# A three-layer decoder kernel: where it waits for the stored queries of its second attention, the order of that stage's first loads, and a wait of the experts' first transposes

## The chip, the cores and the metric

One Trainium2 chip, one core of it. The time is device microseconds (us) of one execution of the whole kernel, one launch. Engines: PE (TensorE), DVE (VectorE), ACT (ScalarE), POOL (GpSimd) and SP (SyncE, which here only issues DMAs and waits). The measured times of the kernel before are three, 1827.96 to 1846.97 us, so a difference below about 1% can hardly be told from none.

## The reference

`x` is 4 x 1024 tokens of 256 values, `ctx` is 4 x 77 tokens. All arithmetic is float32.

```python
x = layernorm(x + attn(x, ...))            # 16 heads of 16, rotary, ALiBi: causal bias only, softmax over 1024 keys
x = layernorm(x + xattn(x, ctx, mask, ...))
x = layernorm(x + ffn(x, ...))             # router, top 2 of 8 experts, 1024 places each, hidden 1024

def xattn(q, k, v, mask, ...):             # k = v = ctx
    qh, kh, vh = heads(q @ Wq.T + bq), heads(k @ Wk.T + bk), heads(v @ Wv.T + bv)
    scores = einsum('bhqd,bhkd->bhqk', qh, kh) / sqrt(16) + mask * -1e15
    return heads_back(softmax(scores) @ vh) @ Wo.T + bo

def ffn(x, ...):
    ids, probs = top2(relu(x @ rw1 + rb1) @ rw2 + rb2)
    disp = rows of x, sorted to their experts' places
    h = relu(einsum('enc,ech->enh', disp, ew1) + eb1)
    return sum over both experts of probs * (einsum('enh,ehc->enc', h, ew2) + eb2)
```

## The kernel before

The kernel is seven stages, one behind the other, each a block of five instruction streams, one for each engine. At the end of a block every engine drains (line 49 in the profile) and all wait for all; the next stage's instructions start behind that. Semaphores order everything else by hand: `eng.wait_ge(sem, value)` holds back all that follows on that engine, and a DMA raises its semaphore by 16 when it has landed.

The stages of the 4096 tokens: projections (`stage_qkv`), self attention, `stage_self_out` (output projection, norm, and the queries and keys of the second attention), `stage_cross` (the second attention, its projection and norm), router, `stage_experts`, `stage_combine`. From `stage_self_out` on they work in 8 chunks of 512 tokens.

**Queries through DRAM.** `stage_self_out` splits each chunk's queries into a high and a low part (`q_hi`, `q_lo`) and SP stores both to `q2_scr` (`store_q`, line 1156; the profile calls the tensor `q_scr`). Their landings are counted by `q_out[n % 2]`, 32 for each chunk. The x1 rows are stored at line 1151 (`x1_out`). The second attention loads a chunk's queries as a stack: `load_query_side` (line 1049) brings rows 0 to 47 of one half of the partitions, SP the one half and ACT the other. There are 4 such stacks; 0 and 1 are loaded in `stage_self_out` already. Each stack also has rows of ones (`load_ones`, line 1056, 64 KB a DMA, counted by `ones_in`).

**The second attention's start.** Scores are made twice. First `max_pairs` (line 1804): half a tile's heads each, 8 for a chunk, into PSUM, and DVE takes maxima (line 1708). When a chunk's 8 are there, DVE makes the negated maxima as two float parts (`shifts`), PE transposes them (line 1813), ACT copies them to `neg_t` (`copy_top`, line 1647), and SP moves them through DRAM to two rows of the query stack (`move_top`: store at line 1594, then loads at 1598). Only then can PE make that chunk's true scores (`scores`, line 1824), with the shift as rows of the product. Ahead of the main loop PE makes 14 such halves (`LEAD`), all of chunk 0 and 6 of chunk 1. The main loop then goes in 8 steps a chunk, with a `max_pairs` in each until all are made. SP's stream in the loop loads stack n + 3, x1 of chunk n (for the residual), moves the shift of n + 1 and stores chunk n - 2.

**The experts' start.** The router's last act on SP is to load the first two blocks of sorted rows (`first_rows`). In `stage_experts` SP loads the biases `eb1` (`b1`) and the constant `spare`, both counted by `const_in`. PE transposes the first rows (line 2465), ACT and DVE split them (2343, 2379), DVE works out shares and homes with `spare` (`shares`), and PE's products follow (2477). `b1` is first read by ACT's relus.

Of the kernel before, what the change touches and what calls it, by code (L numbers as in the profile page):

```python
# [13 lines left out]
F32R = mybir.dt.float32r  # L14
# [7 lines left out]
P = 128  # L22
# [4 lines left out]
CK = C // P  # L27
CH = 512
TPC = CH // P
CHUNKS = T // CH  # L30
# [85 lines left out]
PAIRS = H // 2  # L116
# [918 lines left out]
def cross_tiles(s):  # L1035

    return {"k_max": s.sb("k_max", [P, PAIRS, B, LP], F32R), "k_exp": s.sb("k_exp", [P, PAIRS, B, L], F32R),
            "v_all": s.sb("v_all", [L, B, H, VP], F32), "key_bias": s.sb("key_bias", [L, B], F32),  # L1040
            "stacks": [s.sb(f"q_stack{i}", [P, PAIRS, CH], F32R) for i in range(2)]}


def load_query_side(eng, io, n, side, stack):

    src = io["q2_scr"][n].rearrange("r (j s) t -> s r j t", s=2)[side]
    for row, first, last in ((0, 0, 2 * D), (2 * D, 0, D)):
        at = 64 * side + row
        eng.dma_start(stack[at:at + last - first, :, :].bitcast(F32), src[first:last]).then_inc(io["chunk_in"][n], 16)
# [12 lines left out]
Q_STORES = 32  # L1062
# [5 lines left out]
def stage_self_out(nc, io, pre, lent):  # L1068

    with Scope(nc, "so") as s:  # L1070
# [9 lines left out]
        q_sum = [s.sb(f"q_sum{i}", [P, CK, CH], F32) for i in range(2)]  # L1080
        q_hi = [s.sb(f"q_hi{i}", [P, CK, CH], F32R) for i in range(2)]
        q_lo = [s.sb(f"q_lo{i}", [P, CK, CH], F32R) for i in range(2)]
        norm = Norm(nc, s, io["apart"])
# [15 lines left out]
        spare = stacks[1][:, :, :].rearrange("p j t -> p (j t)")  # L1099
        wk_hi, wk_lo = [spare[:, i * 2048:(i + 1) * 2048].rearrange("p (c m) -> p c m", c=CK) for i in range(2)]  # L1100
        t_ps = s.pb("t_ps", (P, CK, CH))
        r_ps = s.pb("r_ps", (P, TPC, C))
# [8 lines left out]
        ones_in = lent["ones_in"]  # L1111
# [7 lines left out]
        x1_out = [s.sem(f"x1_out{i}") for i in range(2)]  # L1119
        q_out = [s.sem(f"q_out{i}") for i in range(2)]  # L1120
        block = s.block()
# [13 lines left out]
        def _(sp):  # L1135
# [44 lines left out]
            for c in range(2):  # L1180
                sp.wait_ge(x1_out[c], 16 * CHUNKS // 2)
                sp.wait_ge(q_out[c], Q_STORES * CHUNKS // 2)

# [335 lines left out]
def stage_cross(nc, io, pre, lent):  # L1519


    with Scope(nc, "cr") as s:
# [36 lines left out]
        x2_done = s.sem("x2_done")  # L1559
        ones_in = lent["ones_in"]  # L1560
        out_done = s.sem("out_done")
# [16 lines left out]
        def _(sp):  # L1578
            def load_stack(n):
                if n >= Q_SETS:  # L1580
                    sp.wait_ge(s_done, H * (n - Q_SETS) + H)
                load_query_side(sp, io, n, 0, qst[n % Q_SETS])

# [17 lines left out]
            def store(n):  # L1601
# [3 lines left out]
                sp.dma_start(chunk_rows(io["x2_scr"][0:T], n), x2[n % 2][:, :, :]).then_inc(out_done, 16)  # L1605

            load_stack(2)
            for i in (2, 3):
                load_ones(sp, io, qst[i], ones_in)
            load_x(0)  # L1610
            move_top(0)
            sp.dma_start(bo, io["bo"].partition_broadcast(P)).then_inc(weights_in, 16)
# [28 lines left out]
        def _(act):  # L1641
# [28 lines left out]
            def load_stack(n):  # L1670
                if n >= Q_SETS:
                    act.wait_ge(s_done, H * (n - Q_SETS) + H)
                load_query_side(act, io, n, 1, qst[n % Q_SETS])

# [27 lines left out]
        def _(dve):  # L1702
# [42 lines left out]
            for h in range(LEAD):  # L1745
                maxima(h)
                if h == HALVES - 1:
                    shifts(0)
            dve.wait_ge(hi_done, 1)
            nc.vector.tensor_tensor(wo_lo[:, :, :], wo_raw, wo_hi[:, :, :].bitcast(F32), ALU.subtract).then_inc(lo_done, 1)  # L1750
            for n in range(CHUNKS + 2):
                for u in range(HALVES):
                    h = HALVES * n + u + LEAD
# [28 lines left out]
        def _(pe):  # L1782
# [8 lines left out]
            def max_pairs(h):  # L1791
                n, q, b, t, first = max_half(h)
                if h % HALVES == 0:
                    pe.wait_ge(q_in[n], STACKED)
                    if n == 2:
                        pe.wait_ge(ones_in, 128)
                if 2 <= h < LEAD:
                    pe.wait_ge(m_free, h - 1)
                elif h >= LEAD:
                    pe.wait_ge(m_free, h)  # L1800
                for j in range(HG):
                    for side in range(2):
                        rows = slice(64 * side, 64 * side + ROWS_MAX)
                        ins = nc.tensor.matmul(max_bank(h)[:, side, j * LP:(j + 1) * LP], q[rows, first + j, t * P:(t + 1) * P],  # L1804
                                               k_max[rows, first + j, b, :], start=True, stop=True)
                ins.then_inc(m_full, 1)
# [416 lines left out]
def stage_experts(nc, io, keep):  # L2223

    with Scope(nc, "ex") as s:
# [100 lines left out]
        def _(act):  # L2326
            act.sem_inc(relu_done, 2)
            act.wait_ge(const_in, 32)

# [37 lines left out]

            split_x(0, 0)
            for e in range(E):
                expert(e, e % 2, e == E - 1)  # L2370

        @block.vector
        def _(dve):
# [7 lines left out]
            def shares(h, c):  # L2381
                e, at = h // 2, SHARE_STEPS * h
                who, home_of = rows[c][:, :, C:C + 1], rows[c][:, :, C + 2:C + 3]
                dve.wait_ge(in_done[c], 16 * e + 16)
                dve.wait_ge(ratio_done, h + 1)
                if h >= 4:
                    dve.wait_ge(added, 64 * (h - 3))
# [67 lines left out]
        def _(pe):  # L2455
            pe.sem_inc(h_done, 16)
            pe.wait_ge(const_in, 32)

# [316 lines left out]
```

## Time and profile before

| | us |
|---|---|
| median of 3 executions | 1835.07 |
| lowest, highest | 1827.96, 1846.97 |
| the profiled execution, its own time | 1830.21 |
| its span, first to last instruction | 1828.4 |
| second attention, first to last product of PE (about 1022 to 1220) | some 200 |
| experts (about 1394 to 1784) | some 390 |

The span is what the trace covers, 1.8 us less than that execution's own time. PE is busy for 89% of the span, but the stages differ, and a chain that ended last says little here, since it reaches back only into the last stage. So the two joints between stages that the change touches are read from the timelines.

### The profile page before, as it was taken

The numbers are of one execution on the slowest core, as the hardware profiler recorded it, in microseconds if no ns is written. First come the engines' busy times: TensorE is split into PE (matmuls) and PEld (weight loads), VectorE is DVE, ScalarE is ACT, GpSimd is POOL, SyncE is SP. The second block draws the span as 40 slices with busy tenths as digits, with TensorE's granted clock in tenths as the row PEclk, the third lists the DMA queues.
The fourth block names the chain that finished last, engine by engine and source line by source line (L and its number), as shares of the span: only waits on it lengthen the run. The fifth ranks groups of instructions, "written<-read, shape, count | busy, mean of one in ns | idle before, by whom it ended". The sixth has DMA issues, their size and how long they took to land. (4 is left out here: it accounts for less than half of the span.)

```text
span 1828.4 us, 36172 instructions
## 1 busy us (share of the span) xinstructions
PE 1623.4 (89%) x14816; PEld 1061.1 (58%) x14816; DVE 1278.5 (70%) x2240; ACT 1006.9 (55%) x1727; POOL 387.6 (21%) x265
## 2 busy tenths in 40 slices
PE   7869999999999999999777599869984999999990
PEld 6734444444444444444366455547763888888890
DVE  6978888888888888888177446752333677777744
ACT  5326777777777777777635267844532233333313
POOL 6550000000000000000014001101452355555521
PEclk9968999999999999999889578978996999999995
DMA  7955444443433343420238866223213244434226
GB/s 240 259 168 95 93 93 91 91 90 90 98 84 65 63 69 69 69 39 9 78 125 239 191 96 122 68 86 110 84 39 114 70 96 96 96 96 96 39 24 195
DMA packets 130388, 184.36 MB, mean 101 GB/s; under 512 B 29466, under 2 KB 93736, under 8 KB 129132
## 3 DMA queue, kind: packets, MB, share of 16 engines
q1 hardware_dynamic: 113456, 153.70, 34.0%
q0 software_dynamic: 13440, 22.07, 5.8%
q10 hardware_dynamic: 3328, 6.29, 2.1%
q8 instruction: 117, 1.92, 0.5%
q14 instruction: 47, 0.39, 0.1%
HBM read 115.32 MB, written 70.06 MB: 101 GB/s over the span
## 5 line engine op out<-in xcount | busy, mean ns | idle before, releaser
L734 DVE TENSOR_REDUCE att_row_max<-att_ring 128x2 f32<-128x1024 f32 x512 | 601.7, 1220 | 108.4 <-PE att_ring L799 76.4
L718 ACT ACTIVATE att_w_exp<-att_s_ps 128x512 f32<-128x512 f32 x1008 | 539.2, 598 | 210.1 <-PE att_s_ps L846 140.3
L873 PE MATMUL att_a_ps<-att_w_exp,att_v_group 128*32 128x512 f32 x2048 | 273.6, 606 | 0.8 <-ACT att_acc_sb L707 0.6
L832 PE MATMUL att_s_ps<-att_q_stack,att_k_stack 62*128 62x512 f32 x640 | 183.8, 478 | 0.0
L832 PEld LDWEIGHTS att_s_ps<-att_q_stack,att_k_stack 62*128 62x128 f32 x640 | 86.2, 184 | 122.2 <-ACT att_w_exp L718 111.9
L2357 ACT ACTIVATE ex_hid<-ex_h_ps,ex_b 128x512 f32<-128x512 f32 x128 | 87.4, 686 | 116.7 <-DVE ex_h_lo L2412 66.5
L2412 DVE TENSOR_TENSOR ex_h_lo<-ex_hid,ex_h_hi 128x512 fp32r<-128x512 f32 x128 | 138.6, 1083 | 4.4
L648 POOL COPY att_eyes<-keep_slope_eye 128x384 bf16<-128x384 bf16 x16 | 8.1, 507 | 622.6 <-PE att_s_ps L846 613.7
L2307 POOL DMA_INDIRECT x_scr<-ex_y,ex_home x60 | 100.6, 1677 | 176.0 <-DVE ex_y L2402 162.3
L846 PE MATMUL att_s_ps<-att_eyes,keep_past_bf 64*128 64x64 bf16 x3786 | 131.8, 193 | 0.0
L799 PE MATMUL att_ring<-att_k_stack,att_q_stack 60*128 60x512 f32 x640 | 125.6, 439 | 5.0 <-DVE att_row_max L734 4.1
L832 PE MATMUL att_s_ps<-keep_q_stack,keep_k_stack 62*128 62x512 f32 x368 | 109.4, 487 | 1.7 <-ACT att_w_exp L718 1.2
L846 PEld LDWEIGHTS att_s_ps<-att_eyes,keep_past_bf 64*128 64x128 bf16 x3786 | 92.1, 95 | 29.7 <-issue 17.7
L1656 ACT ACTIVATE cr_e<-cr_score_ps,pre_key_bias 77x512 f32<-77x512 f32 x128 | 80.5, 679 | 40.6 <-PE cr_score_ps L1824 39.8
L799 PE MATMUL att_ring<-keep_k_stack,keep_q_stack 60*128 60x512 f32 x384 | 85.6, 487 | 18.3 <-DVE att_row_max L734 8.9
L2343 ACT ACTIVATE ex_x_hi<-ex_t_ps 128x1024 fp32r<-128x1024 f32 x16 | 16.4, 1028 | 139.7 <-PE ex_t_ps L2465 139.7
L832 PEld LDWEIGHTS att_s_ps<-keep_q_stack,keep_k_stack 62*128 62x128 f32 x368 | 50.4, 188 | 73.9 <-ACT att_w_exp L718 67.8
L2410 DVE CAST ex_h_hi<-ex_hid 128x512 fp32r<-128x512 f32 x128 | 71.9, 562 | 15.8 <-ACT ex_hid L2357 15.1
L2420 DVE TENSOR_TENSOR ex_y<-ex_y_ps,ex_b 128x256 f32<-128x256 f32 x64 | 25.4, 420 | 80.5 <-PE ex_y_ps L2488 80.5
L1708 DVE TENSOR_REDUCE cr_top<-cr_m_ps 128x8 f32<-128x616 f32 x57 | 45.4, 797 | 48.8 <-PE cr_m_ps L1804 48.4
L807 PEld LDWEIGHTS att_ring<-att_eyes,keep_past_bf 64*128 64x128 bf16 x1280 | 35.1, 98 | 67.2 <-issue 67.2
L2488 PE MATMUL ex_y_ps<-ex_w_hi,ex_h_lo 128*128 128x256 f32 x256 | 72.9, 285 | 0.0
(314 smaller groups left out, 3552.6 us busy)
## 6 DMA issues: line engine op xcount, KB each, us to landing
first_w_raw<-ew SPq DMA_DIRECT2D x16, 1024.0 KB
att_k_stack<-qk_scr SPq DMA_DIRECT2D x40, 256.0 KB
rows_scr<-att_zeros POOLq DMA_DIRECT2D x8, 1040.0 KB, 9.3
first_rows<-rows_scr SPq DMA_DIRECT2D x16, 520.0 KB
qk_scr<-qkv_t_lo SPq DMA_DIRECT2D x14, 512.0 KB, 4.7
qk_scr<-qkv_t_hi SPq DMA_DIRECT2D x14, 512.0 KB, 4.4
keep_k_stack<-qk_scr SPq DMA_DIRECT2D x24, 256.0 KB
att_q_stack<-qk_scr SPq DMA_DIRECT2D x20, 256.0 KB
```

What stands on the lines that cost most here:

```text
L718: nc.scalar.activation(w_exp[(STEPS * g.n + st) % SETS][h][:, :], score_bank(v), ACT.Exp).then_inc(exp_done, 1)
L734: nc.vector.tensor_reduce(out, ring[place.slot][:, :, :], AX.X, ALU.max).then_inc(ring_free, 1)
L799: return nc.tensor.matmul(ring[place.slot][:, i, :], qs[g.buf][rows, j, tok:tok + P], ks[g.buf][rows, half, j, kk * CH:(kk + 1) * CH], sta ...
L832: ins = nc.tensor.matmul(score_bank(v), ks[g.buf][rows, c, j, kt * P:(kt + 1) * P], qs[g.buf][rows, j, c * CH:(c + 1) * CH], start=True, s ...
L846: ins = nc.tensor.matmul(bank[:, at:at + 64], past[side, far, half, :], eyes[g.buf][side, part, h // 2, :], start=False, stop=n == last)
L873: ins = nc.tensor.matmul(a_ps[32 * h:32 * h + 32, :], vg[g.buf][:, kt, h * VW:h * VW + 32], w_exp[(STEPS * g.n + st) % SETS][h][:, :], sta ...
L1656: nc.scalar.activation(e[p % E_SETS][:, side, :], s_ps[v % S_BANKS][0:L, :], ACT.Exp, bias=key_bias[:, n // 2:n // 2 + 1]).then_inc(exp_do ...
L2307: pool.indirect_dma_start(io["x2_scr"], bass.IndirectOffsetOnAxis(home[h % 4][:, t, :], 0), y[c][:, t, :], None, compute_op=ALU.add).then_ ...
L2357: nc.scalar.activation(hid[m % 2][:, :], h_ps[m % 2][:, :], ACT.Relu, bias=b1[:, bass.ds(e, 1), m:m + 1].rearrange("p a b -> p (a b)") if ...
L2410: nc.vector.tensor_copy(h_hi[c][:, m, :], hid[m % 2][:, :]).then_inc(h_hi_done, 1)
L2412: nc.vector.tensor_tensor(h_lo[c][:, m, :], hid[m % 2][:, :], h_hi[c][:, m, :].bitcast(F32), ALU.subtract).then_inc(h_lo_done, 1)
L2488: ins = nc.tensor.matmul(y_ps[t][:, 0:C], a, b, start=(j == 0), stop=(j == len(prods) - 1))
```

## The change

Four things, in two stages.

1. `q_out` is made in `cross_tiles` and lives on in the second attention. `stage_self_out` no longer ends with a wait of SP for it; instead SP and ACT wait for it in `load_stack`, for the chunk that they load, and DVE waits for all of it once, ahead of `wo_lo`. `q_hi` and `q_lo` stand later in the list of buffers, so that what the second attention writes first does not lie on them.
2. On SP, at that stage's start, the ones of stack 2 and `move_top(0)` stand ahead, and the ones of stack 3 and x1 of chunk 0 behind them.
3. PE waits for the ones of stacks 2 and 3 apart.
4. In `stage_experts` PE no longer waits for `const_in`; ACT waits for it behind its first split, DVE in `shares`.

```diff
@@ cross_tiles
-            "stacks": [...]}
+            "stacks": [...],
+            "q_out": [s.sem(f"q_out{i}") for i in range(2)]}
@@ stage_self_out
-        q_hi = [s.sb(f"q_hi{i}", [P, CK, CH], F32R) for i in range(2)]
-        q_lo = [s.sb(f"q_lo{i}", [P, CK, CH], F32R) for i in range(2)]
...
+        q_hi = [s.sb(f"q_hi{i}", [P, CK, CH], F32R) for i in range(2)]
+        q_lo = [s.sb(f"q_lo{i}", [P, CK, CH], F32R) for i in range(2)]
...
             for c in range(2):
                 sp.wait_ge(x1_out[c], 16 * CHUNKS // 2)
-                sp.wait_ge(q_out[c], Q_STORES * CHUNKS // 2)
@@ stage_cross, SP (ACT's load_stack alike)
             def load_stack(n):
                 if n >= Q_SETS:
                     sp.wait_ge(s_done, H * (n - Q_SETS) + H)
+                sp.wait_ge(q_out[n % 2], Q_STORES * (n // 2 + 1))
                 load_query_side(sp, io, n, 0, qst[n % Q_SETS])
...
+            load_ones(sp, io, qst[2], ones_in)
             load_stack(2)
-            for i in (2, 3):
-                load_ones(sp, io, qst[i], ones_in)
+            move_top(0)
+            sp.wait_ge(ones_in, 96)
+            load_ones(sp, io, qst[3], ones_in)
             load_x(0)
-            move_top(0)
@@ stage_cross, DVE
                 if h == HALVES - 1:
                     shifts(0)
+
+            for c in range(2):
+                dve.wait_ge(q_out[c], Q_STORES * CHUNKS // 2)
             dve.wait_ge(hi_done, 1)
@@ stage_cross, PE, max_pairs
-                    if n == 2:
-                        pe.wait_ge(ones_in, 128)
+                    if n in (2, 3):
+                        pe.wait_ge(ones_in, 32 * n + 32)
@@ stage_experts
             act.sem_inc(relu_done, 2)
-            act.wait_ge(const_in, 32)
...
             split_x(0, 0)
+            act.wait_ge(const_in, 32)
...
                 dve.wait_ge(ratio_done, h + 1)
+                if h == 0:
+                    dve.wait_ge(const_in, 32)
...
             pe.sem_inc(h_done, 16)
-            pe.wait_ge(const_in, 32)
```

The order on SP's queue, from the last store of queries over the end of the stage (the two branches) into the second attention. `cr_q_stack` are stacks 2 and 3, `pre_q_stack` stacks 0 and 1. Before:

```order
L1156 DMA q_scr<-so_q_lo 128x2x512
L49 UNCONDITIONAL_BRANCH [waits so_x1_out1,so_q_out0,so_q_out1,so_x1_out0,lent_ones_in]
L1577 UNCONDITIONAL_BRANCH [waits barrier_Pool_Activation_PE_DVE_SP_release]
L1049 DMA cr_q_stack<-q_scr 32x8x512
L1049 DMA cr_q_stack<-q_scr 16x8x512
L1056 DMA cr_q_stack<-ones_scr 4x4096 x4
L1589 DMA cr_x<-x_scr 128x4x256
L1594 DMA shift_scr<-cr_neg_t 32x512 [waits cr_top_copied]
L1598 DMA pre_q_stack<-shift_scr 2x4096 [waits cr_top_out]
L1598 DMA pre_q_stack<-shift_scr 2x4096
L1612 DMA lent_att<-bo 128x256
L1049 DMA cr_q_stack<-q_scr 32x8x512
```

and in the changed kernel (whose lines have numbers of their own):

```order
L1158 DMA q_scr<-so_q_lo 128x2x512
L49 UNCONDITIONAL_BRANCH [waits so_x1_out1,so_x1_out0,lent_ones_in]
L1578 UNCONDITIONAL_BRANCH [waits barrier_Pool_Activation_PE_DVE_SP_release]
L1057 DMA cr_q_stack<-ones_scr 4x4096 x2
L1050 DMA cr_q_stack<-q_scr 32x8x512 [waits pre_q_out0]
L1050 DMA cr_q_stack<-q_scr 16x8x512
L1596 DMA shift_scr<-cr_neg_t 32x512 [waits cr_top_copied]
L1600 DMA pre_q_stack<-shift_scr 2x4096 [waits cr_top_out]
L1600 DMA pre_q_stack<-shift_scr 2x4096
L1057 DMA cr_q_stack<-ones_scr 4x4096 [waits lent_ones_in]
L1057 DMA cr_q_stack<-ones_scr 4x4096
L1591 DMA cr_x<-x_scr 128x4x256
L1615 DMA lent_att<-bo 128x256
```

The waits for the queries' stores have left the stage's end, and the shift's store has moved ahead of two ones loads and of x1's load.

The order on PE where the experts begin, before:

```order
L2454 UNCONDITIONAL_BRANCH [waits barrier_Pool_Activation_PE_DVE_SP_release]
L2465 MATMUL ex_t_ps<-lent_ident,first_rows 128x128 [waits first_rows_in0,ex_const_in]
L2465 MATMUL ex_t_ps<-lent_ident,first_rows 128x128 x7
L2465 MATMUL ex_t_ps<-lent_ident,first_rows 128x128 [waits ex_x_lo_done,first_rows_in1]
L2465 MATMUL ex_t_ps<-lent_ident,first_rows 128x128 x7
```

and in the changed kernel:

```order
L2463 UNCONDITIONAL_BRANCH [waits barrier_Pool_Activation_PE_DVE_SP_release]
L2473 MATMUL ex_t_ps<-lent_ident,first_rows 128x128 [waits first_rows_in0]
L2473 MATMUL ex_t_ps<-lent_ident,first_rows 128x128 x7
L2473 MATMUL ex_t_ps<-lent_ident,first_rows 128x128 [waits ex_x_lo_done,first_rows_in1]
L2473 MATMUL ex_t_ps<-lent_ident,first_rows 128x128 x7
```

Nothing has changed its place; the first transpose waits for the rows alone.

## Rows read from the trace of the kernel before

**Rows 1.** The page's first line.

```profile
span 1828.4 us, 36172 instructions
```

**Rows 2.** Timeline of SP: start us, us, line, operation (instructions in a row).

```profile
1015.21 0.47 SPq L1156 DMA_DIRECT2D q_scr<-so_q_lo  x1
1022.06 1.22 SPq L1049 DMA_DIRECT2D cr_q_stack<-q_scr  x2
...
1025.05 0.39 SPq L1589 DMA_DIRECT2D cr_x<-x_scr  x1
1033.02 0.32 SPq L1594 DMA_DIRECT2D shift_scr<-cr_neg_t  x1
1040.67 0.53 SPq L1598 DMA_DIRECT2D pre_q_stack<-shift_scr  x2
...
1041.65 1.20 SPq L1049 DMA_DIRECT2D cr_q_stack<-q_scr  x2
...
1093.80 0.31 SPq L1594 DMA_DIRECT2D shift_scr<-cr_neg_t  x1
...
1118.75 0.33 SPq L1594 DMA_DIRECT2D shift_scr<-cr_neg_t  x1
...
1139.13 0.33 SPq L1594 DMA_DIRECT2D shift_scr<-cr_neg_t  x1
```

**Rows 3.** Timeline of PE and ACT: in brackets idle before, and its releaser.

```profile
1022.10 1.08 PE L1804 MATMUL cr_m_ps<-pre_k_max,pre_q_stack 52*128 52x78 f32 x8 [13.28 <-PEq L49]
...
1032.40 0.59 ACT L1647 ACTIVATE cr_neg_t<-cr_turn_ps 32x512 fp32r<-32x512 f32 x1 [18.89 <-PE cr_turn_ps L1813]
...
1038.21 1.07 PE L1804 MATMUL cr_m_ps<-pre_k_max,pre_q_stack 52*128 52x78 f32 x8 [0.90 <-DVE cr_top L1708]
...
1044.86 0.71 PE L1824 MATMUL cr_score_ps<-pre_q_stack,pre_k_exp 50*77 50x512 f32 x2 [5.57 <-DMA pre_q_stack<-shift_scr]
```

**Rows 4.** Waits of SP, 1000 to 1024 us: total, times, longest.

```profile
SPq L1181 <- DMA q_scr<-so_q_lo: 3.4, 1, 3.4
...
SPq L1182 <- DMA q_scr<-so_q_lo: 2.5, 1, 2.5
```

**Rows 5.** Landings of the last x1 store (L1151), issued at 1000.5.

```profile
DMA to landing us min/median/max: 9.2/9.2/9.2
```

**Rows 6.** Line 49, a stage's end: 1012 to 1023, then 1380 to 1392.

```profile
L49 DVEq DRAIN  x1: 1258/1258/1258, 1013.6 to 1013.6; - x1
...
L49 POOLq DRAIN  x1: 5284/5284/5284, 1386.2 to 1386.2; - x1
```

**Rows 7.** Landings of the shift's stores (L1594), and of x loads (L1589).

```profile
DMA to landing us min/median/max: 2.2/5.1/7.6
...
DMA to landing us min/median/max: 3.6/8.2/15.4
```

**Rows 8.** DMA queue q1, 1038 to 1041: packets, MB, share of 16 engines.

```profile
q1 hardware_dynamic: 112, 0.11, 11.8%
```

**Rows 9.** Timeline of SP and PE where the experts begin.

```profile
1391.77 0.35 SPq L2263 DMA_DIRECT2D ex_b<-eb  x1
1392.17 0.42 SPq L2264 DMA_DIRECT2D ex_spare<-spare  x1
...
1394.02 1.97 PE L2465 MATMUL ex_t_ps<-lent_ident,first_rows 128*128 128x128 f32 x8 [22.66 <-DMA ex_spare<-spare]
```

**Rows 10.** Windows: length, five engines busy, then granted clock, DMA share, GB/s.

```profile
1013.00:1016.00 3.00, 0.00 (x0) 0.00 (x0) 1.23 (x1) 0.52 (x1) 0.00 (x0) 0.50 1.01 222
...
1073.00:1076.00 3.00, 3.00 (x30) 1.47 (x27) 1.16 (x2) 1.89 (x4) 1.35 (x1) 0.84 0.85 90
1094.00:1097.00 3.00, 3.00 (x19) 1.32 (x20) 1.58 (x7) 1.94 (x4) 0.00 (x0) 0.57 1.06 109
1106.00:1109.00 3.00, 3.00 (x22) 2.27 (x24) 1.17 (x3) 0.31 (x1) 2.25 (x1) 0.65 0.49 174
1391.00:1391.70 0.70, 0.00 (x0) 0.00 (x0) 0.00 (x0) 0.00 (x0) 0.00 (x0) 0.50 0.00 0
```

More of the change, by code:

```diff
@@ L1040, in cross_tiles @@
             "v_all": s.sb("v_all", [L, B, H, VP], F32), "key_bias": s.sb("key_bias", [L, B], F32),
-            "stacks": [s.sb(f"q_stack{i}", [P, PAIRS, CH], F32R) for i in range(2)]}
+            "stacks": [s.sb(f"q_stack{i}", [P, PAIRS, CH], F32R) for i in range(2)],
+            "q_out": [s.sem(f"q_out{i}") for i in range(2)]}
 def load_query_side(eng, io, n, side, stack):
@@ L1119, in stage_self_out @@
         x1_out = [s.sem(f"x1_out{i}") for i in range(2)]
-        q_out = [s.sem(f"q_out{i}") for i in range(2)]
+        q_out = pre["q_out"]
         block = s.block()
@@ L1559, in stage_cross @@
         x2_done = s.sem("x2_done")
-        ones_in = lent["ones_in"]
+        ones_in, q_out = lent["ones_in"], pre["q_out"]
         out_done = s.sem("out_done")
@@ L1672, in load_stack @@
                     act.wait_ge(s_done, H * (n - Q_SETS) + H)
+                act.wait_ge(q_out[n % 2], Q_STORES * (n // 2 + 1))
                 load_query_side(act, io, n, 1, qst[n % Q_SETS])
```

## The prediction

> **What bounds the kernel now.** The chain that ended last covers only the last stage, so I went by the two joints that the change touches. At each I read, in this order, which engine waits and for whom, the timeline across the joint, and then the queue of the engine that was named.
>
> The first joint is the start of the second attention. SP has issued its last store of queries at 1015.21 + 0.47 = 1015.68 [rows 2]. It then waits 3.4 us and 2.5 us for stores of queries [rows 4], to 1021.6, and its first DMA of the next stage is at 1022.06: 0.45 us from the end of its waits to the start of the stage. PE has stood idle 13.28 us by then [rows 3]. PE makes the 14 leading halves until 1038.21 + 1.07 = 1039.28, and then stands idle 5.57 us, until 1044.86, for the shift of chunk 0 [rows 3]. That shift left ACT at 1032.40 + 0.59 = 1032.99, SP stored it at 1033.02, and went on to the loads only at 1040.67 [rows 2, 3]: 7.6 us for 64 KB, the longest of its eight stores; the median is 5.1, the shortest 2.2 [rows 7].
>
> The second joint is the start of the experts. All engines are released at about 1391.7, SP issues `spare` at 1392.17, and PE's first transpose starts at 1394.02, released by `spare` [rows 9], which it doesn't read.
>
> **The end of the first stage.** What holds the stage's end when SP no longer waits for queries? The last x1 store was issued at 1000.5 and took 9.2 us, to 1009.7 [rows 5]. DVE, with the last work of all, has drained at 1013.6 + 1.26 = 1014.9 [rows 6]. So SP itself is last, at 1015.68, and the second attention starts at 1015.68 + 0.45 = 1016.1, which is **5.9 us** earlier. The leading halves need chunks 0 and 1 only, whose stacks were loaded a stage earlier. The PE clock doesn't profit from the shorter idle time: the granted clock is down to half, 1.2 GHz, in 1013 to 1016 already [rows 10], so PE makes the leading halves as slowly as before, and ends them at 1039.28 - 5.93 = 1033.35.
>
> **The shift of chunk 0.** ACT's copy and SP's store move with the start, to 1033.02 - 5.93 = 1027.1. Then the store's landing. Before, it stood behind stack 2, four loads of ones and x1 of chunk 0, issued at 1025.05 [rows 2], which took 15.4 us [rows 7], to 1040.5: it landed with the shift's store, at the same tail. Now only stack 2 and two loads of ones stand ahead, but the stage starts while the last stores of queries, issued up to 1015.68, are still landing (until 1021.6 before). The time that the store takes here is not in the trace. Its bounds are the shortest and the longest of the eight, 2.2 and 7.6. I take the median, 5.1, since the store again stands behind a stack's load, as most of the eight do. It lands at 1027.1 + 5.1 = 1032.2. From there to PE's first score it was 1044.86 - 1040.67 = 4.2 us, and still is, as the ones and x1 come behind those loads. First score at 1036.4, against 1044.86: **8.5 us** earlier in all, of which 5.9 are the stage's start and 2.6 the queue. With 2.2 us PE would be ready before the shift, nearly: 1033.5, 11.4 us earlier. With 7.6 us it is 1038.9, 6.0 us earlier.
>
> Ones loads bring 4 rows each, the store 32. In 1038 to 1041, at the end of that tail, queue q1 keeps 11.8% of 16 engines busy [rows 8], so about two of them: the tail is uneven. By the Trainium skill (page "DMA: Bandwidth & Descriptors", section "Why a DMA increments its semaphore by 16 and not by 1"), a DMA from SP is split over the largest number of engines, up to 16, that divides the slowest dimension, which for 4 rows is four engines, the lowest ones. By that the ones are what the store waits for, not x1, and half of them still stand ahead: half of the excess of 7.6 over 2.2 would stay, and the store would take 4.9 us. By the queue alone, with x1 and the ones of stack 3 gone, 2.2 us could be reached.
>
> **What the moved steps cost.** x1 of chunk 0, `bo` and stack 3 now come behind the shift's second wait on SP, so at about 1032.5 to 1035, against 1025 to 1042.9. POOL and DVE need x1 only in chunk 0's residual, more than 20 us later, and PE needs stack 3 and its ones after ten further halves, also over 20 us after the first score. Stack 3 is even issued a little ahead of the first score, as before (1041.65 against 1044.86, [rows 2]). All added waits for `q_out` find their stores landed: chunk 2's and 3's are several chunks old, and DVE's wait for all stands behind the leading maxima, at some 1032, where the last stores were down at 1021.6 before. Each costs an instruction's time on an engine that isn't the bound. Moving `q_hi` and `q_lo` among the buffers runs nothing.
>
> **The experts.** The transposes go at the release, about 1391.75, instead of 1394.02: **2.2 us** (2.27 less a little). What is late next? Not the rows: nothing moves on the DMA engines any more from 1391.0 to 1391.7 [rows 10], ahead of the release, which comes with the end of POOL's drain, 1386.2 + 5.3 = 1391.5 [rows 6]. ACT's wait for `const_in` now stands behind the first split (PE 1.97 us, then ACT), which ends past 1394, and so costs nothing. DVE's `shares` come later still. PE is bound to stay busy through the experts, so the 2.2 us last to the end.
>
> **Sum.** 8.5 + 2.2 = 10.7 us. Both stages behind run relative to these starts, and nothing there waits for a time of its own. Span 1828.4 [rows 1] to 1817.7; the execution's own time 1830.21 to 1819.5; the median, 4.9 us above that execution, 1835.07 to **1824.4 us**, 0.6% less.
>
> **The rivals.**
> *The queue eats the reordering.* Stack 2 and the stores of queries share the engines, and the shift's store takes 7.6 us or more. For it: q1 is full while the stores land. Against: the store comes eleven microseconds after the start. Gain 6.0 + 2.2 = 8.2: 1826.9 us.
> *The change doesn't bring the start forward.* Something else holds the stage's end, as POOL's drain of 5.3 us did at the router's [rows 6]. Here all drains that I see are over at 1014.9, so this is unlikely. Gain 2.2 and at most 2.6: about 1832.
> *The clock rises earlier.* PE got its full clock, 2.4 GHz, only at about 1073, fell to half at about 1094.5 and rose again at about 1107 [rows 10]. The chunk with those 12.5 us of half clock took 1118.75 - 1093.80 = 24.95 us from shift to shift, the next 1139.13 - 1118.75 = 20.38 [rows 2]: 0.37 us for each us at half clock. With the gap of 5.57 us mostly closed, PE works without a break from the start. If one such stretch goes, 4.6 us more are gained, 1819.8; with two, 1815.2.
> *The clock stays low, and the kernel is slower.* The same price the other way: the second attention has other gaps and a changed beat, and PE may be granted half a clock through further chunks. From 10.7 / 0.37 = 29 us of additional half clock the kernel is slower than before; with 50 us it loses 18.3 and ends at 1842.7. Against it: the order of PE's work is the same, and the two falls before followed idle time.
>
> **How the numbers follow.** The forecast, with the bounds of the shift's store inside it (1821.5 to 1826.9), 0.55; the crowded queue 0.15; the start not brought forward 0.06; the earlier clock 0.15; the later clock 0.09. The three runs lie 7 us below and 12 above their median, so a median may be some 7 us off by itself. The range goes from the earlier clock less a part of that spread, 1811, to the middle of the late one's, 1837. A difference under 1% is about what a measurement of this kernel can't tell from none; faster by more needs 1816.7, which takes the earlier clock or a lucky median, 0.18; slower by more needs 1853.4, 0.04; the rest 0.78.
>
> **What would show it.** In the changed profile: SP's line 49 wait gone and its first DMA 0.5 us after the last store was issued; PE's idle time ahead of the first half 7.4 us instead of 13.3; the shift's store with 5 us, and PE idle about 3 us ahead of its first score; the experts' first transpose within 0.1 us of the release. I am wrong if the stage starts later than DVE's drain and SP's issue allow, if the shift's store takes over 8 us, or if the windows show another course of the clock: that decides more than any of the terms.

## The result: 0.5% faster, as large as forecast, but not by the terms of the sum

| 15 executions each | before | changed |
|---|---|---|
| median, us | 1832.89 | 1824.51 |
| lowest to highest | 1827.96 to 1846.97 | 1819.15 to 1833.51 |
| the profiled execution's span | 1828.4 | 1827.7 |

The ratio is 0.9948, with a 95% interval of 0.9928 to 0.9968: 9.5 us (6 to 13) by the ratio, against 10.7 forecast. The profiled execution of the changed kernel took 1829.48 us, 5 above its median, and shows a gain of 0.7 us only, so places in the two traces can be compared, the spans can't. Part of that is ahead of the change: the last store of queries is issued at 1018.07 here and at 1015.68 before. One execution of the kernel before (4936.76 us) and one of direct (1984.2 us), both taken with the experiments below, were far slower than all others and are left out of the ratios.

SP's timeline of the changed kernel, against [rows 2] (start, duration, line, what, instructions in a row):

```profile
1017.60 0.47 SPq L1158 DMA_DIRECT2D q_scr<-so_q_lo  x1
1018.58 1.35 SPq L1057 DMA_DIRECT2D cr_q_stack<-ones_scr  x2
...
1029.54 0.32 SPq L1596 DMA_DIRECT2D shift_scr<-cr_neg_t  x1
1033.88 0.53 SPq L1600 DMA_DIRECT2D pre_q_stack<-shift_scr  x2
1034.45 0.59 SPq L1057 DMA_DIRECT2D cr_q_stack<-ones_scr  x2
1035.08 0.39 SPq L1591 DMA_DIRECT2D cr_x<-x_scr  x1
1035.51 0.51 SPq L1615 DMA_DIRECT2D lent_att<-bo  x1
1036.06 1.21 SPq L1050 DMA_DIRECT2D cr_q_stack<-q_scr  x2
1045.43 0.32 SPq L1596 DMA_DIRECT2D shift_scr<-cr_neg_t  x1
1058.50 0.54 SPq L1600 DMA_DIRECT2D pre_q_stack<-shift_scr  x2
```

The stage starts at 1018.58, 0.51 us after that store was issued (forecast 0.45). The shift's store takes 1033.88 - 1029.54 = 4.3 us (7.6 before, 5.1 forecast). The ones of stack 3, x1, `bo` and stack 3 follow right behind its loads, and then comes what I had not foreseen: the second shift's store, at 1045.43, is through only at 1058.50, after 13.1 us. Before, the same took 1055.52 - 1050.59 = 4.9:

```profile
1050.59 0.31 SPq L1594 DMA_DIRECT2D shift_scr<-cr_neg_t  x1
1055.52 0.54 SPq L1598 DMA_DIRECT2D pre_q_stack<-shift_scr  x2
```

The landings of these stores say the same (before: [rows 7], 7.6 at most):

```profile
DMA to landing us min/median/max: 2.1/4.9/13.1
```

On PE, against [rows 3]:

```profile
1018.62 1.07 PE L1811 MATMUL cr_m_ps<-pre_k_max,pre_q_stack 52*128 52x78 f32 x8 [7.88 <-PEq L49]
...
1034.74 1.07 PE L1811 MATMUL cr_m_ps<-pre_k_max,pre_q_stack 52*128 52x78 f32 x8 [0.90 <-DVE cr_top L1712]
1039.70 0.71 PE L1831 MATMUL cr_score_ps<-pre_q_stack,pre_k_exp 50*77 50x512 f32 x2 [3.89 <-DMA pre_q_stack<-shift_scr]
...
1062.12 0.71 PE L1831 MATMUL cr_score_ps<-pre_q_stack,pre_k_exp 50*77 50x512 f32 x2 [2.47 <-DMA pre_q_stack<-shift_scr]
```

PE stood idle for 7.88 us, not 13.28, ahead of the second attention. From the last store's issue to its first score are 39.70 - 18.07 = 21.6 us, against 44.86 - 15.68 = 29.2: 7.6 us won, of 8.5 forecast. But the second leg, from the loads' issue to the score, grew from 4.2 to 5.8 us, and the second shift now stops PE for 2.47 us, where before it stopped nobody. The course of the clock is another as well (windows; after POOL's busy time the granted clock, DMA share, GB/s), against [rows 10]:

```profile
1073.00:1076.00 3.00, 3.00 (x19) 1.07 (x11) 0.45 (x2) 1.59 (x3) 0.00 (x0) 0.50 0.10 22
1085.00:1088.00 3.00, 3.00 (x23) 2.24 (x25) 0.59 (x1) 0.49 (x2) 0.00 (x0) 0.69 0.00 0
1094.00:1097.00 3.00, 1.87 (x18) 1.19 (x14) 2.83 (x8) 1.26 (x2) 0.00 (x0) 1.00 1.06 184
1106.00:1109.00 3.00, 3.00 (x29) 1.78 (x28) 2.10 (x5) 2.21 (x5) 2.00 (x1) 1.00 0.42 151
```

Before, half clock ended at about 1073 and came back from 1094.5 to 1107. Here it lasts until about 1086.5, in the second chunk's steps, and doesn't come back in the third. From the issue of the second shift's store to that of the sixth's it is 93.0 us, against 88.5 before: 4.5 us of the 7.6 are given back there. By the first scores of the chunks, the first chunk takes 22.4 us (19.7 before), the second 27.5 (21.1), the third 20.4 (24.9). So some 2.7 of it go to the first chunk, where the new wait is, and some 1.9 to the clock, which costs 6.4 in the second chunk and gives 4.5 back in the third.

Where the experts begin, against [rows 9]:

```profile
1390.80 0.34 SPq L2270 DMA_DIRECT2D ex_b<-eb  x1
...
1390.99 1.94 PE L2473 MATMUL ex_t_ps<-lent_ident,first_rows 128*128 128x128 f32 x8 [20.79 <-PEq L49]
1391.19 0.43 SPq L2271 DMA_DIRECT2D ex_spare<-spare  x1
```

The transpose starts 0.19 us after SP's first issue, not 2.25, and PE doesn't wait for `spare`, which is issued behind it. The stage's first product follows 6.18 us after that issue, where it was 8.33: 2.15 us of 2.2 forecast.

### The profile page after: what moved, and what is told of

It is laid out like the page before. It is cut to its first block and busy times, and to the rows that moved or that the text cites. A ratio compares the mean times of both kernels' runs of the same rounds, so it can differ in the third digit from the quotient of the medians.

```text
span 1827.7 us, 36179 instructions
## 1 busy us (share of the span) xinstructions
PE 1630.1 (89%) x14816; PEld 1065.5 (58%) x14816; DVE 1280.7 (70%) x2240; ACT 1007.0 (55%) x1727; POOL 388.8 (21%) x265
## 5 line engine op out<-in xcount | busy, mean ns | idle before, releaser
L2421 DVE TENSOR_TENSOR ex_h_lo<-ex_hid,ex_h_hi 128x512 fp32r<-128x512 f32 x128 | 138.6, 1083 | 4.4
```

The lines of the kernel that those rows point to most:

```text
L2421: nc.vector.tensor_tensor(h_lo[c][:, m, :], hid[m % 2][:, :], h_hi[c][:, m, :].bitcast(F32), ALU.subtract).then_inc(h_lo_done, 1)
```

## The experiments

All are compared with the kernel before, run on the same chip, by 9 to 12 executions each (15 of the changed kernel, 6 of direct_fill, one of x_ahead and one of ones_ahead). The traces are of one execution each. Shifts have the numbers of their chunks, from 0: the first shift is shift 0, and the last column runs from the issue of the second shift's store to that of the sixth's. "Store" is the time from the issue of the shift's store to the issue of the loads behind it, "leg 2" from there to the first score.

| kernel | ratio to before (95%) | median us | store / leg 2 | PE's waits for shifts 0 and 1 | shift 1 to 5, us |
|---|---|---|---|---|---|
| before | 1 | 1831.5 to 1833.0 | 7.6 / 4.2 | 5.6, 0 | 88.5 |
| changed | 0.9948 (0.9928 to 0.9968) | 1824.51 | 4.3 / 5.8 | 3.9, 2.5 | 93.0 |
| start_only | 0.9967 (0.9944 to 0.9990) | 1825.61 | 7.1 / 4.0 | 4.8, 0 | 88.6 |
| queue_only | 1.0005 (0.9981 to 1.0029) | 1832.77 | 4.8 / 5.1 | 3.6, 3.1 | 93.9 |
| experts_only | 0.9996 (0.9978 to 1.0014) | 1832.83 | 8.5 / 3.6 | 5.9, 0 | 91.7 |
| hold_loads | 0.9956 (0.9939 to 0.9973) | 1825.71 | 4.7 / 3.6 | 2.0, 2.8 | 93.7 |
| top_first | 0.9956 (0.9932 to 0.9980) | 1823.20 | 4.1 / 3.1 | 0.9, 0 | 91.6 |
| old_order | 0.9966 (0.9941 to 0.9991) | 1823.88 | 6.9 / 4.3 | 4.9, 0 | 91.7 |
| x_ahead | one execution | 1821.80 | 6.0 / 5.9 | 5.6, 0.8 | 91.6 |
| ones_ahead | one execution | 1827.01 | 5.8 / 4.8 | 4.6, 0 | 90.5 |
| direct | 0.9934 (0.9904 to 0.9964) | 1823.10 | 7.6 in all | 1.4, 0 | 95.7 |
| fill_end | 0.9966 (0.9941 to 0.9991) | 1825.89 | 5.4 / 4.9 | 4.1, 2.8 | 93.2 |
| fill_gap | 0.9944 (0.9917 to 0.9970) | 1825.33 | 5.6 / 5.2 | 0, 3.3 | 94.7 |
| direct_fill | 0.9913 (0.9882 to 0.9944) | 1819.06 | 7.7 in all | 1.5, 0 | 95.7 |

**start_only: the early start alone.**

```diff
 (the changed kernel's waits for q_out; SP's first loads and the experts as before)
             load_stack(2)
             for i in (2, 3):
                 load_ones(sp, io, qst[i], ones_in)
             load_x(0)
             move_top(0)
```

> Only the waits for stored queries are moved; the order of SP's first loads and the experts' waits are those of before. Theory (my sum): the start of the second attention moves 5.9 us ahead, but the shift's store of chunk 0 still stands behind four loads of ones and x1, and these now share the engines with the last stores of queries: the store takes 9 to 12 us instead of 7.6, PE's idle time ahead of its first score grows to 7 to 9 us, and 1 to 5 us are left of the 5.9 (ratio 0.997 to 0.9995). Rival: what counts is the start, the queue is never the limit; then the store takes 7.6 us and all 5.9 us show (ratio 0.9968).

Its timeline of SP, and its waits of PE (total, times, longest):

```profile
1025.54 0.32 SPq L1596 DMA_DIRECT2D shift_scr<-cr_neg_t  x1
1032.59 0.53 SPq L1600 DMA_DIRECT2D pre_q_stack<-shift_scr  x2
```

```profile
PE cr_m_ps L1810 <- PEq L49: 7.2, 1, 7.2
...
PE cr_score_ps L1830 <- DMA pre_q_stack<-shift_scr: 4.8, 1, 4.8
```

My theory fell. The stores of queries that are still landing don't delay the shift: its store takes 7.05 us, no more than before. PE's first score comes 22.6 us after the last store's issue, 6.6 us sooner than before (5.9 from the start, the rest from the store), and the ratio is what 5.9 us give, with an interval of 1.8 to 10 us.

**queue_only: the new order alone.**

```diff
 (the changed kernel, with the stage's end and the experts as before)
                 sp.wait_ge(x1_out[c], 16 * CHUNKS // 2)
+                sp.wait_ge(q_out[c], Q_STORES * CHUNKS // 2)
```

> Only the order of SP's first loads is changed (with the split wait of PE for the ones); the stage before still waits for all stores of queries, and the experts' waits are those of before. Theory: the start stays, the shift's store takes about 4 to 5 us instead of 7.6 and PE's idle time ahead of its first score falls from 5.6 to 2 or 4 us: 2 to 4 us gained (ratio 0.998 to 0.999). Rival, that the order does nothing without the earlier start: store 7.6 us, ratio 1.000.

```profile
PE cr_m_ps L1812 <- PEq L49: 13.2, 1, 13.2
PE cr_score_ps L1832 <- DMA pre_q_stack<-shift_scr: 6.7, 2, 3.6
```

Both expectations are half right. The first shift's wait fell from 5.6 to 3.6 us; but there are two waits, 6.7 us together, and by the ratio (an interval of some 4 us either way) the kernel is as fast as before. The order wins 2 us at the first shift and loses 3.1 at the second.

**experts_only.**

```diff
-            act.wait_ge(const_in, 32)      # ACT, at its start
...
             split_x(0, 0)
+            act.wait_ge(const_in, 32)
...
+                if h == 0:
+                    dve.wait_ge(const_in, 32)
...
-            pe.wait_ge(const_in, 32)
```

> Only the waits for the biases in the experts are moved. Theory: first transpose at the release instead of 2.2 us behind it, and PE's products 2.2 us earlier to the end: ratio 0.9988. Rival, that another wait or the clock takes the gain: ratio 1.000, with the first product of the experts not earlier against the release.

Its timeline at the release:

```profile
1396.27 0.34 SPq L2263 DMA_DIRECT2D ex_b<-eb  x1
...
1396.46 1.94 PE L2466 MATMUL ex_t_ps<-lent_ident,first_rows 128*128 128x128 f32 x8 [20.74 <-PEq L49]
```

The transpose again starts 0.19 us after the first issue. The time, 0.9996 with an interval of 0.0018 either way, holds both 2.2 us and nothing; that the 2.2 us reach the end is seen at the start of the products only, not in the total.

**hold_loads: nothing behind the first shift until it has landed.**

```diff
             sp.wait_ge(ones_in, 96)
+            sp.wait_ge(top_in[0], 32)
             load_ones(sp, io, qst[3], ones_in)
```

> The changed kernel with one more wait on SP: the ones of stack 3, x1 and stack 3 are issued only when the shift of chunk 0 has landed in the query stack. In the changed kernel the shift's second leg took 5.8 us (issue to first score) where before it took 4.2. Theory, that what is issued right behind it slows it: the leg falls back to 4.2 us or less and PE's idle time from 3.9 to about 2.3 us (ratio to the changed kernel 0.999). Rival, that it is slow for another reason, such as stack 2 still landing: the leg stays at 5 to 6 us and nothing is gained.

```profile
PE cr_score_ps L1832 <- DMA pre_q_stack<-shift_scr: 4.8, 2, 2.8
```

Two waits, the longest 2.8 us and so 2.0 for the other one. Leg 2 is 3.6 us instead of 5.8: what is issued right behind the shift's loads slows them. The table says the same of the ones: leg 2 is 4.9 to 5.9 us where ones are issued right behind these loads (changed, queue_only, x_ahead, fill_end), and 3.1 to 4.8 where they are not (fill_gap and direct can't be compared). The second wait stays, 2.8 us, and the total can't be told from the changed kernel's.

**top_first: both shifts ahead of the bulk.**

```diff
             load_ones(sp, io, qst[2], ones_in)
             load_stack(2)
             move_top(0)
+            move_top(1)
             sp.wait_ge(ones_in, 96)
             load_ones(sp, io, qst[3], ones_in)
+            load_stack(3)
             load_x(0)
             sp.dma_start(bo, ...)
 (and neither load_stack(3) nor move_top(1) in the loop's first round)
```

> The changed kernel, but on SP the shifts of chunk 0 and of chunk 1 both go ahead of the ones of stack 3, SP's half of stack 3, x1 of chunk 0 and bo. In the changed kernel the second shift's store stood behind all of these and took 13.1 us (4.9 before), PE waited 2.5 us for it, and its clock rose only at about 1088, 26 us behind that wait. Theory, that this queue took back what the first shift won: the second shift's store takes 2 to 4 us, PE waits only once (2 to 4 us, ahead of the first score), and the clock rises one 12 to 16 us stretch earlier: 2.5 to 8 us less than the changed kernel, ratio 0.990 to 0.9935. Rival, that the clock's course does not hang on that wait: only 2.5 to 4 us less, ratio 0.9925 to 0.9935, and the clock rises at the same step of chunk 2 as in the changed kernel.

```profile
1039.96 0.31 SPq L1596 DMA_DIRECT2D shift_scr<-cr_neg_t  x1
1043.69 0.52 SPq L1600 DMA_DIRECT2D pre_q_stack<-shift_scr  x2
...
1065.44 0.50 SPq L1596 DMA_DIRECT2D shift_scr<-cr_neg_t  x1
1078.30 0.54 SPq L1600 DMA_DIRECT2D cr_q_stack<-shift_scr  x2
```

```profile
1034.24 0.71 PE L1833 MATMUL cr_score_ps<-pre_q_stack,pre_k_exp 50*77 50x512 f32 x2 [0.86 <-DMA pre_q_stack<-shift_scr]
...
1059.64 1.07 PE L1813 MATMUL cr_m_ps<-pre_k_max,cr_q_stack 52*128 52x78 f32 x8 [1.62 <-DMA cr_q_stack<-q_scr]
```

The second shift's store takes 3.7 us, and PE's wait for it is gone: so the queue of bulk ahead of it was its cause (which part of the bulk, ones_ahead shows below). But PE now waits 1.62 us for stack 3, which comes later, and the third shift's store, behind the next stack and x1, takes 12.9 us. The bulk has moved on by one chunk. The clock rises at about 1080, 46 us after the first score, as in the changed kernel (1086.5 - 39.7 = 47): on the clock the rival was right. The gain beyond the changed kernel is 1.3 us by the medians and none by the ratios.

**old_order: all but the new order.** It is start_only with the experts' waits moved.

> The changed kernel with SP's first loads in the order of before (early start and experts' waits kept). Theory, that the new order wins as much at the first shift as it loses at the second and in the clock: no difference to the changed kernel, ratio to before 0.994 to 0.997; the first shift's store 7 us, PE idle 4.8 us ahead of its first score, no wait at the second shift, and the clock rises at about 1066 to 1074. Rival, that the new order is worth its 2.6 us: ratio 0.9965 or more.

Store 6.9 us, one wait of 4.9, clock full from about 1064. The ratio, 0.9966, lies in both expected ranges and so doesn't decide between them; the trace goes as the theory said. The intervals of this kernel and of the changed one overlap, so the new order is worth nothing that can be measured, as in queue_only.

**x_ahead and ones_ahead: what holds the first store up?**

```diff
 x_ahead                                 ones_ahead
             load_stack(2)                           load_stack(2)
+            load_x(0)                               sp.wait_ge(ones_in, 96)
             move_top(0)                +            load_ones(sp, io, qst[3], ones_in)
             sp.wait_ge(ones_in, 96)                 move_top(0)
             load_ones(...)                          load_x(0)
-            load_x(0)
```

> The changed kernel with x1 of chunk 0 back ahead of the first shift's store, the ones of stack 3 still behind it. If x1 holds the store up, it takes about 6 to 7 us instead of 4.3; if the ones do, 4.3 to 5.

> The changed kernel with the ones of stack 3 ahead of the first shift's store (issued once the ones of stack 2 have landed), x1 still behind it. If the ones hold the store up, since by the Trainium skill (DMA: Bandwidth & Descriptors, Why a DMA increments its semaphore by 16 and not by 1) their 4 rows go over four engines only, it takes about 6 to 7 us instead of 4.3; if x1 does, 4.3 to 5.

Their timelines of SP:

```profile
1025.15 0.33 SPq L1596 DMA_DIRECT2D shift_scr<-cr_neg_t  x1
1031.11 0.53 SPq L1600 DMA_DIRECT2D pre_q_stack<-shift_scr  x2
```

```profile
1027.80 0.59 SPq L1057 DMA_DIRECT2D cr_q_stack<-ones_scr  x2
1028.43 0.31 SPq L1596 DMA_DIRECT2D shift_scr<-cr_neg_t  x1
1034.26 0.52 SPq L1600 DMA_DIRECT2D pre_q_stack<-shift_scr  x2
...
1045.61 0.32 SPq L1596 DMA_DIRECT2D shift_scr<-cr_neg_t  x1
1051.77 0.54 SPq L1600 DMA_DIRECT2D pre_q_stack<-shift_scr  x2
```

The store takes 5.96 us behind x1 and 5.83 behind the ones: each adds about 1.5 us to 4.3, and both together make the 7 us of start_only. x1 is 512 KB, the two loads of ones 128 KB, so a byte of ones costs four times a byte of x1. (The ones are issued 0.6 us ahead of the store, x1 8.4 us, so the comparison is not a clean one.) The Trainium skill (DMA: Bandwidth & Descriptors, Why a DMA increments its semaphore by 16 and not by 1) has 4 rows on four of the 16 engines. The packet records of ones_ahead agree: the eight packets of 16 KB of the two loads run as four pairs, in each the second starting where the first ends (as at 1029.69 and 1030.32). But x1 counts as much in sum.

For the second shift's store the two kernels tell more, and I had overlooked it. In ones_ahead x1, `bo` and stack 3 are issued right behind the first shift just as in the changed kernel, and only the ones are not among them. Its second store takes 1051.77 - 1045.61 = 6.2 us, not 13.1, and PE doesn't wait for it. In x_ahead, where x1 stands ahead of the first store and the ones behind it, the second store takes 11.3 us and PE waits 0.8. So of what the new order put ahead of the second shift, the 128 KB of ones cost it some 7 us, and the 512 KB of x1 some 2. All traces fit: where the ones are issued between the first shift and the second store it takes 11.3 to 13.8 us (changed, queue_only, hold_loads, x_ahead, fill_end, fill_gap), where they are not 3.7 to 6.2 (before, start_only, experts_only, old_order, ones_ahead, top_first). Why ones issued 11 us earlier cost so much is not shown. And though PE has no second wait in ones_ahead, its clock rises late as well, at about 1085, 46 us after the first score.

**direct: the shift without DRAM.**

```diff
-                sp.dma_start(io["shift_scr"][i], neg_t[i][:, :].bitcast(F32)).then_inc(top_out, 16)
-                sp.wait_ge(top_out, 16 * n + 16)
                 for side in range(2):
-                    ... (2 rows from shift_scr)
+                    for part in range(2):
+                        row, at = 64 * side + ROW_SHIFT + part, 2 * PAIRS * part + PAIRS * side
+                        sp.dma_start(qst[n % Q_SETS][row:row + 1, :, :].bitcast(F32),
+                                     neg_t[i][at:at + PAIRS, :].bitcast(F32)).then_inc(top_in[i], 16)
```

> The changed kernel with the shifts moved straight from ACT's tile to the rows of the query stack, four loads of 16 KB each from SBUF to SBUF, instead of a store to DRAM, a wait and two loads. Theory: one leg is gone at each chunk, so PE's idle time ahead of its first score falls from 3.9 us to 0 or 1, and the second shift, though still queued behind stack 3, is down 3 to 5 us sooner, which ends PE's 2.5 us wait there: 4 to 7 us less than the changed kernel, ratio to before 0.991 to 0.993. Rival, that the queue's length and not the number of legs counts: the second wait stays, and 3 us or less are gained, ratio 0.9935 to 0.995.

```profile
1026.26 2.78 SPq L1599 DMA_DIRECT2D pre_q_stack<-cr_neg_t  x4
...
1039.62 2.72 SPq L1599 DMA_DIRECT2D pre_q_stack<-cr_neg_t  x4
```

```profile
PE cr_score_ps L1830 <- DMA pre_q_stack<-cr_neg_t: 1.4, 1, 1.4
```

Issuing the four takes SP 2.78 us, and from the first issue to the first score it is 7.6 us instead of 10.2. One wait is left, 1.4 us, so both waits went as in the theory. That this is faster than the changed kernel is not shown: 0.9934 and 0.9948, with intervals that overlap. In the profiled execution the clock was half for 102 of the 206 us from 1004 to 1210 (79 in the changed kernel), so it took 1830.10 us, where the median is 1823.10.

**fill_end and fill_gap: can idle products keep the clock?** Both add products that nobody reads.

```diff
 fill_end: PE, at the end of stage_self_out, behind the last queries
+            for i in range(24):
+                nc.tensor.matmul(t_ps[:, 0, :], w_hi[:, 1, 0, 0:P], x1_hi[1][:, 0, :], start=True, stop=True)
 fill_gap: PE, between the leading halves and the loop
+            pe.wait_ge(hi_done, 1)
+            for i in range(30):
+                nc.tensor.matmul(a_ps[:, 0:B * L], wo_hi[:, 0, 0:P], k_exp[:, i % PAIRS, :, :]..., start=True, stop=True)
```

> The changed kernel with 24 products of 128x512 that nobody reads, on PE behind its last queries, where it stands idle for 7.9 us before the second attention. They add no path of work. Theory, that the half clock of the second attention's first 60 us comes from that idle time and costs time: PE's clock is still full at the start of the leading halves, they take 2 to 3 us less, and if it stays full through chunks 0 and 1 some 10 us more (ratio 0.987 to 0.994). Rival, that the leading halves by themselves bring the clock down: half again within a few us of their start, the same course as in the changed kernel and the same time.

> The changed kernel with 30 products of 128x308 that nobody reads, on PE between the leading halves and the first score: 7.7 us at half clock, of which 3.9 stand in idle time. Theory, that dense products there raise the clock as they do at the start of the experts: full clock from the first scores on instead of from about 1086, which gives back 8 us or more and wins 4 or more after its own 3.9 (ratio 0.993 or less). Rival, that the clock falls again at once in chunk 0: 2 to 4 us slower than the changed kernel (ratio 0.9965).

PE's timeline of fill_end (eight products of 78 columns a row), and the windows of fill_gap:

```profile
1014.48 0.64 PE L1813 MATMUL cr_m_ps<-pre_k_max,pre_q_stack 52*128 52x78 f32 x8 [2.58 <-PEq L49]
...
1016.01 0.64 PE L1813 MATMUL cr_m_ps<-pre_k_max,pre_q_stack 52*128 52x78 f32 x8 [0.44 <-DVE cr_top L1714]
...
1017.55 1.08 PE L1813 MATMUL cr_m_ps<-pre_k_max,pre_q_stack 52*128 52x78 f32 x8
```

```profile
1026.00:1032.00 6.00, 5.91 (x41) 5.54 (x40) 4.54 (x6) 1.32 (x2) 0.00 (x0) 0.50 0.30 50
...
1034.00:1036.00 2.00, 2.00 (x18) 1.82 (x16) 0.00 (x0) 0.00 (x0) 0.00 (x0) 1.00 0.87 152
1036.00:1040.00 4.00, 2.64 (x32) 1.79 (x33) 2.35 (x5) 2.62 (x5) 0.00 (x0) 1.00 1.07 165
...
1042.00:1044.00 2.00, 2.00 (x12) 0.32 (x10) 0.44 (x1) 1.26 (x2) 0.00 (x0) 0.50 1.06 60
```

In fill_end the halves take 0.64 us at full clock and 1.08 from 1017.55 on: the clock fell while PE was working on them, 3 us into the stage. They were ready 0.9 us sooner, and the total is no better than the changed kernel's. In fill_gap the clock is full from about 1033, while the dense products run, and half again from about 1040, with chunk 0 under way. Both rivals were right, but for fill_gap's price: its products, 6.1 us in the trace, cost nothing that can be measured. In its trace the clock rose at about 1068 instead of 1086, and was half again from about 1095 to 1115; whether this paid for the products is open.

**direct_fill: the two together.**

> Shifts moved straight from SBUF to SBUF, and the 24 idle products behind the last queries, in one kernel. If both theories hold their gains add: ratio 0.985 to 0.990. If the idle products do nothing, it equals the kernel with the straight shifts.

It is the fastest of all, 0.9913, with 6 executions. The interval reaches up to 0.9944 and so meets the changed kernel's and direct's; that it beats them is likely, not shown. Nor does it decide between gains that add (0.985 to 0.990 expected) and idle products that do nothing.

## Why the prediction held, and which steps of it did not

- **The start, 5.9 us: right.** 0.51 us from issue to start, and start_only, with this alone, gives 0.9967, which is 6.0 us (1.8 to 10).
- **The shift's store, 5.1 us with bounds of 2.2 and 7.6: right in size.** It took 4.1 to 5.6 in all kernels with the new order and 6.9 to 8.5 with the old. The rival "the queue eats the reordering" was not what happened at this shift, and the stores of queries turned out to cost nothing. That "the ones are what the store waits for, not x1" was half right: at this store each adds 1.5 us.
- **Leg 2, "4.2 us, and still is": wrong by 1.6 us.** I took what is issued behind a DMA to be behind it. hold_loads shows that it isn't: 3.6 us with nothing behind, 5.8 with the ones, x1, `bo` and stack 3 right behind.
- **"What the moved steps cost": this is the step that failed.** I checked for each moved load who needs it, and found nobody near. I didn't ask what stands behind it on the same queue, and that is the next chunk's shift: 13.1 us instead of 4.9, a new wait of 2.5. queue_only has both waits and no gain; top_first removes the cause, and the wait goes. ones_ahead narrows it down: with the ones alone taken out from behind the first shift, the second store takes 6.2 us and the wait is gone.
- **The experts, 2.2 us: right at the place** (2.15), and neither confirmed nor refuted in the total.
- **The clock.** I gave the earlier rise 0.15, the later one 0.09. With the new order the stores of the third and the fourth shift (in direct, the moves themselves) are 25 us or more apart, and the rise came at 1080 to 1092, in all profiled executions but fill_gap's (19.3 us, 1068); with the old order they are 19.3 to 19.6 us apart, and it came at 1064 to 1074 and fell again in the third chunk. Over shifts 1 to 5 that is 90.5 to 95.7 us against 88.5 to 91.7. With the new wait it takes back what the new order wins. The late rise doesn't hang on that wait: top_first and ones_ahead have no wait for the second shift (top_first has one for stack 3) and their clock rises as late, 46 us after their first score, where the kernels with the old order take 29. What does decide it is open.
- **The sum.** 5.9 from the start, 1.7 from the shift and 2.2 at the experts are 9.7, and the measured 9.5 us seem to be those. But the second wait and the clock stand against them, and start_only and queue_only tell that 6.0 of the 9.5 us come from the early start and none that can be measured from the order. What makes up the other 3.5 is open: the experts' 2.2 and the uncertainty of 3.6 us either way cover it, though old_order, which is the early start and the experts together, shows no more than start_only (0.9966 and 0.9967). So that the number came out this near is in part luck. The median, forecast as 1824.4 and measured as 1824.51, owes more to it: the kernel before came out at 1832.89, not at the 1835.07 that the forecast started from, and the two medians lie 8.4 us apart, not 10.7.

## What to carry to other kernels

A wait at a stage's end holds back everything, so moving it to the one load that needs it is worth its full length; here that was 6 us, and neither racing stores nor added waits took anything from it. When something small and urgent is moved ahead on a DMA queue, list what the bulk then stands in front of, down to the next urgent transfer of the same kind, and not only who reads the bulk. Don't go by bytes alone: here two loads of 4 rows, 128 KB, held the next shift up more than 512 KB of x1. Where one execution's clock is worth 5 us, compare places in traces and medians of many runs, never two spans.

## What the runs showed of the hardware

The time of one execution follows PE's clock closely. In 34 executions of the kernel before, the mean granted clock lies between 0.919 and 0.931 and the time between 1846.03 and 1826.08 us; a straight line through them falls by 1.4 us for each 0.001. Over 1828 us, 0.001 are 3.7 us at half clock, so by an estimate 1 us at half clock costs 0.39 us (0.42 and 0.44 by the 23 and the 26 executions of the two later sets), near the 0.37 that the prediction took from two chunks.

I had thought that idle time brings the clock down in this stage, and fill_end doesn't settle it. PE came to the leading halves, products of 52 rows by 78 columns, at full clock and lost it within 3 us of them, while at work; but it had stood idle for 2.58 us just ahead of them. In the kernel before, the clock fell at about 1094.4, and PE had been idle for 1.1 us of 1091 to 1093. An idle time of the same size, at 1081 to 1083 in old_order, was followed by eight us more at full clock. So idle time stands ahead of these falls, but it is not enough by itself, and whether it is needed is open.

Busy time in the profile doesn't bring the clock back either. This is direct from 1064 to 1088 (length, PE, PEld, DVE, ACT and POOL busy, granted clock, DMA share, GB/s):

```profile
1064.00:1088.00 24.00, 24.00 (x125) 13.42 (x124) 9.32 (x17) 11.54 (x19) 0.00 (x0) 0.50 0.23 41
```

PE is busy for all of the 24 us, at half clock. The Trainium skill (TensorE: Matmul & The Clock Gate, Part 1: The HAM clock gate) has the clock set by how busy PE has been of late. If so, the busy share in the profile is not the measure that it goes by.
